# Second attention: eight batches in a row in every engine's program, in place of a first batch, a loop over six and a last one

## The reference, cut to what matters

```python
x = x + _L0_xattn_ref(_layernorm(x), ctx_1024, ctx_1024, mask, ...)
x = x + _L0_ffn_ref(_layernorm(x), ...)
x = x + _L1_xattn_ref(ctx_1024, _layernorm(x), mask2, ...)
x = x + _L1_ffn_ref(_layernorm(x), ...)

# _L1_xattn_ref, per batch: 256 latents attend to 256 context rows + 256 latents
q = (ln @ Wq)                                  # 16 heads of 64
kv = concat([xn @ Wkv, ln @ Wkv], axis=1)      # 512 keys and values
qn = rmsnorm(q, qn_g) * scale
kn = rmsnorm(k, kn_g)
sim = einsum('bhid,bhjd->bhij', qn, kn)        # masked
attn = softmax(sim)
out = einsum('bhij,bhjd->bhid', attn, v)
return out @ Wout + bout
```

## Time and profile before

| | us |
|---|---|
| median of 3 runs | 1325.49 |
| lowest and highest | 1323.56, 1330.16 |
| profiled execution | 1331.85 |
| its span, first to last instruction | 1330.1 |
| busy in the span: PE, DVE, ACT, POOL | 952.3, 959.7, 771.7, 591.5 |
| second attention, in the span | from about 554 to 1158 |

### The profile page before, as it was taken

The page is one execution under the profiler, slowest core; times in us unless marked ns, Lnnn a source line. Parts: engine busy times, 40 slices in busy tenths (PEclk is TensorE's granted clock), DMA queues, the critical chain, the costliest instruction groups (busy, mean ns, idle before and its releaser), DMA issues. The chain is left out here.

```text
span 1330.1 us, 28004 instructions
## 1 busy us (share of the span) xinstructions
PE 952.3 (72%) x9389; PEld 621.0 (47%) x9394; DVE 959.7 (72%) x1847; ACT 771.7 (58%) x1404; POOL 591.5 (44%) x505
## 2 busy tenths in 40 slices
PE   0378888742999921558887988888788888637655
PEld 0235555521444420125665666666565666514344
DVE  8568989767666668448888787878787887358930
ACT  1227777730555522529988897978787897441022
POOL 8010000021777730537767576767666674220324
PEclk9779999965999965759999999999899999859978
DMA  4311100010000020011111111111111111140140
GB/s 197 87 15 19 22 14 12 1 38 0 24 24 19 11 99 0 1 28 25 27 21 27 25 25 27 25 26 22 22 18 27 19 27 22 51 167 1 38 126 24
DMA packets 73839, 46.72 MB, mean 35 GB/s; under 512 B 55056, under 2 KB 70911, under 8 KB 72646
## 3 DMA queue, kind: packets, MB, share of 16 engines
q1 hardware_dynamic: 72296, 42.40, 13.3%
q0 software_dynamic: 1440, 2.82, 0.6%
HBM read 26.52 MB, written 8.77 MB: 27 GB/s over the span
## 5 line engine op out<-in xcount | busy, mean ns | idle before, releaser
L1385 POOL TENSOR_TENSOR e_p_lo<-e_probs,e_p_hi 128x1024 f16<-128x1024 f32 x64 | 136.3, 2129 | 127.2 <-ACT e_probs L1678 127.2
L1733 DVE TENSOR_REDUCE e_neg_max<-e_row_scores 128x1 f32<-128x512 f32 x256 | 170.1, 683 | 21.3 <-PE e_row_scores L1457 20.8
L1676 ACT ACTIVATE e_p_hi<-e_scores 128x512 f16<-128x512 f32 x256 | 153.1, 598 | 53.0 <-PE e_scores L1561 50.8
L1560 PE MATMUL e_scores<-e_q_stack,e_k_stack 128*128 128x256 f16 x512 | 127.2, 278 | 5.8 <-DVE e_p_lo L1738 5.4
L1368 POOL TENSOR_TENSOR e_raw<-e_raw,e_inv 128x512 f32<-128x512 f32 x96 | 98.9, 1043 | 70.4 <-DVE e_inv L1718 70.4
L1561 PE MATMUL e_scores<-e_q_high,e_k_high 128*128 128x256 f16 x512 | 127.3, 278 | 0.0
L1380 POOL TENSOR_TENSOR e_natural<-e_raw,e_natural 128x512 f16<-128x512 f32 x96 | 109.2, 1157 | 28.2 <-ACT e_natural L1607 27.5
L1457 PE MATMUL e_row_scores<-e_k_high,e_q_high 65*128 65x512 f16 x256 | 96.2, 395 | 33.7 <-DVE e_neg_max L1733 21.8
L716 POOL TENSOR_TENSOR c_h_lo<-c_hidden,c_h_hi 128x512 f16<-128x512 f32 x68 | 78.9, 1160 | 78.0 <-ACT c_h_hi L835 75.8
L1473 PE MATMUL e_mix<-e_v_cols,e_p_hi 128*128 128x65 f16 x1024 | 109.5, 194 | 4.4 <-POOL e_p_lo L1385 3.3
L1474 PE MATMUL e_mix<-e_v_cols,e_p_hi 128*128 128x64 f16 x1024 | 109.6, 196 | 0.0
(11 more groups left out here) (367 smaller groups left out, 2877.1 us busy)
## 6 DMA issues: line engine op xcount, KB each, us to landing
e_k_high<-e_k_stack SPq DMA_DIRECT2D x64, 128.0 KB, 2.7
e_q_high<-e_q_stack SPq DMA_DIRECT2D x32, 128.0 KB, 2.6
w<-in_w SPq DMA_DIRECT2D x2, 2048.0 KB, 10.1
c_w<-in_w SPq DMA_DIRECT2D x17, 192.0 KB, 2.4
placed_scratch<-in_no_rows SPq DMA_DIRECT2D x1, 2313.0 KB, 18.2
a_mask_q<-in_mask_q SPq DMA_DIRECT2D x1, 2048.0 KB, 10.2
a_mask_k<-in_mask_k SPq DMA_DIRECT2D x1, 2048.0 KB, 14.6
parts_scratch<-a_parts SPq DMA_DIRECT2D x2, 1024.0 KB, 4.0
```

The costliest lines, as they stand in the source:

```text
L1385: nc.gpsimd.tensor_tensor(p_lo[buf][i][:], probs[i][:], p_hi[buf][i][:], ALU.subtract).then_inc(lo_done[i], 1)
L1560: pe.matmul(out, k_stack[hf][:, h, cols], q_stack[hf][:, h, :], start=(kt % 2 == 0), stop=False, skip_group_check=True)
L1676: act.activation(p_hi[p % 2][i][:, at, :], scores[n % SBANKS][:], ACT.Exp).then_inc(exp_done, 1)
L1733: dve.tensor_reduce(neg_max[buf][:, 2 * i + qt:2 * i + qt + 1], row_scores[qt % RBANKS][:], AX.X, ALU.max, negate=True).then_inc(max_done, 1)
```

## The change

`flow` is written as a Python loop, so that every engine's program holds all eight batches one behind the other. `b` is a Python number in all of them, and every wait and address is a constant. Nothing is changed in what a batch does or in `ORDER`. Lines behind L1300 move up by two (L1457 becomes L1455).

```diff
         def flow(engine, program):
 
-            program(Batch(0, first=True))
-            with engine.Fori(1, B - 1) as b:
-                program(Batch(b))
-            program(Batch(B - 1, last=True))
+            for b in range(B):
+                program(Batch(b, first=b == 0, last=b == B - 1))
```

## The result

Over the four runs of each kernel measured with the change, the median fell from 1327.83 to 1312.82 us, a ratio of 0.9893 with a 95% interval of 0.9851 to 0.9935 (the ratios of this document, with their intervals, are as measured and differ a little from the quotient of two medians, here 0.9887). Beside the experiments it was timed again over more runs (18 of the kernel before, 6 of the changed one): 1326.75 to 1307.40 us, a ratio of 0.9866 (0.9832 to 0.9901). The forecast was 1307.5 us, a ratio of 0.9864.

The account below looks back on a forecast made before the run. PE and DVE were each busy 72% of the span, with PE's sequencer standing still about 4.2 us at five branches. Saving 18.5 less 0.5 gave 18.0 us, taking the median 1325.49 to 1307.5 us, range 1299 to 1316.

Parts of the forecast that it names:

- The branches: Second attention's loop: removing PE's five long branches back saves 18.5 us, between 5.8 and 23.2.
- The register work: Second attention's loop: 38 us of PE sequencer work in six passes is hidden; removing it loses 0.5 us.
- the four steps: Steps 4 to 8 of a batch, constants against registers: 33.01 us in the first batch, 32.93 in the second.
- Rival four: Register work in steps 1 to 3 was on the path; a third of 38 us back, about 1295; chance 0.05.
- Fetching: Longer programs of the other engines: 25 more q14 packets, costing 0 more time.
- Behind the attention: After the barrier ending the second attention: all that follows moves forward, unshortened and unlengthened.
- The clock: PE's granted clock in the loop, 1.00 then 0.98: no term, already inside the 72.9 us pass.
- (one): PE's stall let DVE, ACT and POOL finish work, so most is given back: 1319.7 or 1310.3 us; chance 0.08.
- (two): PE's long branch is a trace mark no engine pays for: time stays at 1325.5 us; chance 0.03.
- (three): Straight code waits for late instruction blocks, one per batch costing 25 us in all: 1332.7 us; chance 0.04.

Follow-up runs that it names:

- all but PE: Kernel before with SP, ACT, DVE and POOL written out while PE keeps its loop: 1326.63 us, ratio 0.9994.
- the loop moved by 64 and by 256: Kernel before with 32 or 128 small matmuls (64 or 256 instructions) added at PE's very start: 1331.24 and 1327.12 us.
- moved by 160: Kernel before, all loops kept, with 80 small matmuls (160 instructions) added at PE's very start: 1307.86 us, ratio 0.9837.
- The pairs: Kernel before with all engines looping over three pairs, two batches in the body, waits on registers: 1315.31 us, ratio 0.9917.
- the longer first loop: Kernel before with 96 small matmuls more in a pass of the first attention's loop on PE: 1325.40 us in one run.
- the shorter bodies: Kernel before, second attention without the exponentials-high by values-low product for all or half the queries: 1304.66 and 1308.79 us.

## Why the prediction was right

*The branches* were put at 18.5 us, between 5.8 and 23.2. With PE alone written out the ratio gives 17.0 us, and the end of the attention in the changed kernel's profile came 17.2 us earlier. From ACT's rows a pass behind a branch lost 3.7 us and the batches now have 69.24 us. The step of using the lengths of whole passes, and not the branch's 4.2 us or an engine's idle time, gave the right size: DVE's 1.16 us would have said 5.8. How close it came is partly luck. Of the profiles with five stalls, the one that it was taken from has the cheapest: five passes behind a branch took 364.5 us there, and 367.1 to 368.1 in the three others (all but PE, and the loop moved by 64 and by 256). By those the term would have been about 21 to 22 us, and the kernel moved by 160 did gain 20.6 us by the medians and 21.7 by the ratio, against 15.0 and 14.2 in the first measurement of the changed kernel and 19.4 and 17.8 in the second.

*The register work* was put at nothing for its removal, with 0.5 us to pay. The pairs show batches on registers at 69.1 us and the changed kernel has 69.24 on constants; the loss is 0.14 us a batch, about 0.8 in all, and the four steps that I compared beforehand showed it rightly (33.01 against 32.93, then 33.02 and 33.00). All but PE written out gained nothing, and the loop moved by 160 had the whole gain with every engine's register work in place. Rival four is out.

*Fetching* was put at nothing, and rightly in time. In the count I was off: q14 brought 12 packets more and not 25, since I had counted pass one's 5 packets, with its register instructions. Without them two middle batches brought 3 and 2 (654 to 723 us and 861 to 930).

*Behind the attention* nothing was gained or lost by the change: the last part took 170.8 us in one profile and 166.3 in the other of the same kernel, and 172.6 before. The first ratio, 0.9893, is nearer to 1 than the forecast; its interval holds 0.9864, and the repeated measurement gives 0.9866.

*The clock* needed no term of its own: 1.00 in the middle batches, as expected. But the prediction names 0.98 in the fourth pass, and the fifth had 0.95. Of the 3.7 us that a pass lost on average, about 1 is beyond what the one stalled pass at the full clock lost; it was inside the term because whole passes were used.

*Rivals:* that the stall was cover for others (one) or a mark in the trace only (two) is refuted by the passes in four kernels without it: 69.1 us with PE alone written out, with the longer first loop and with the loop moved by 160, and 69.2 in the changed kernel; that straight code starves (three) by the batches written out, with one exception of 0.3 us: one batch of the changed kernel, the one that ended at 861.3 us, took 69.5 us in place of 69.2, with two q14 packets just before. The second profile of the kernel has the same batch at 69.5 us, with two packets at the same place, so it is no accident; that the packets are its cause isn't shown.

*What was incomplete is the cause.* The prediction told the slow loop, with 754 matmuls in a pass, from the fast one, with 693, by its size, and so did the expectations of the shorter bodies. The size matters only through the blocks that it touches. It made no difference for this forecast, since written-out code has no branch back, but it would have misled a reader with the next loop.

What isn't shown: why 7 and not 8. I counted places from the first instruction of the compiled program; a few instructions placed ahead of it on the chip would shift the count, by at most 46 without contradicting a row here.

## What to carry to other kernels

Look at the branch back of each engine's loop in the trace: here 0.05 to 0.24 us is one that finds its target, 4 us one that doesn't, and the length of a pass with and without it says what it costs. Before writing a loop out, count the blocks of 256 instructions that PE's body touches, in the compiled program and with the waits that stand by themselves; here moving the loop by 160 instructions gave the same gain as writing out eight batches, 1307.9 against 1307.4 us (each beside its own measurement of the kernel before, 1328.5 and 1326.8). The reverse holds too: any edit ahead of a long loop can move it across that limit, and then 4 us a pass come or go that have nothing to do with what was edited, so check the branch in both traces before a gain is credited to the edit.

## What the runs showed of the hardware

PE's branch back takes 207 to 243 ns when the body touches 7 blocks of 16 KB and 3.3 to 4.7 us when it touches 8 or 14, in eleven cases over nine kernels. In the fast case q8 brings nothing in the later passes; in the slow one it brings the whole body again in each. Around the first slow branch back of the kernel before, from 725.9 to 730.3 us, it brought two blocks:

```profile
q8 instruction: 2, 0.03, 2.7%
```

The stall doesn't grow with the body beyond that (3.8 to 4.1 us with 14 blocks), and it was the same with the other engines looping or written out (4.2 to 4.6 and 3.7 to 4.7 us). Behind it the granted clock often fell: the passes with a stall had 1.00 once, else 0.98 or 0.95, and those of the second attention without one had 1.00.

The Trainium skill, in "Runtime: NRT & Kernel Launch", section "Instruction fetch mechanics", gives PE 128 KiB, refilled in blocks of 16 KiB, which makes eight blocks. An estimate from that page would be that a body in eight blocks stays. The traces show that it doesn't and that one in seven does; this would fit if one block is always being filled ahead, which no run here shows.

Work on registers ahead of a wait, 6.3 us of PE's sequencer in a batch, was hidden whole: the batches on registers were even 0.1 us shorter.
